# A third table for the last capped expert's rows, cleared in an earlier layer

## The reference, cut to what matters

```python
logits = jnp.einsum('bsh,eh->bse', x, router_w) + router_b        # 8 experts, 2 chosen per token
...
sorted_indices = jnp.argsort(-expert_mask, axis=0)[:cap]          # the first cap = 512 tokens of each of 7 experts
...
h = jax.nn.relu(jnp.einsum('ceh,ehi->cei', inputs, experts_inter))
out = jnp.einsum('cei,eih->ceh', h, experts_out) * in_w[..., None]
combined = jnp.zeros_like(x_flat).at[used_idx].add(out.reshape(-1, hidden))
combined = combined + x_flat * (noop_w * noop_mask)[:, None]      # expert 8 passes the token through
```

## Time and profile before

| | us |
|---|---|
| median of 3 timed runs (1227.82 to 1232.71) | 1228.27 |
| the profiled execution | 1217.18 |
| its span in the trace | 1215.4 |
| route stage, DVE's first to last instruction | 1086.63 to 1109.16 |
| capped mixture, first matmul to the end | 1110.16 to 1215.4 |
| busy in the span: PE, DVE, ACT, GpSimd | 1111.4, 997.1, 855.4, 663.5 |

### The profile page before, as it was taken

How to read it: one execution, slowest core, us unless ns; L and a number is a source line. 1 busy time by engine, 2 the same in 40 slices (tenths; PEclk the granted TensorE clock), 3 DMA queues, 4 the chain that set the end, 5 groups by cost and what they waited for, 6 DMA issues and landing times. The chain is left out here.

```text
span 1215.4 us, 33457 instructions
## 1 busy us (share of the span) xinstructions
PE 1111.4 (91%) x11747; PEld 625.7 (51%) x11747; DVE 997.1 (82%) x2703; ACT 855.4 (70%) x1830; POOL 663.5 (55%) x695
## 2 busy tenths in 40 slices
PE   4999999999999998999999998999999999937975
PEld 2344444444444444666666555655566666523752
DVE  3899999999899896689988899778999999865224
ACT  1688888888888888655556555587889999824314
POOL 3234434554333330556556567667878888735763
PEclk9999999999999999999999999998999999966998
DMA  4111111111111110000000000001122112114217
GB/s 121 32 38 40 40 39 42 41 37 40 38 42 41 43 30 14 2 2 2 1 2 1 2 2 6 24 19 47 35 53 57 53 47 55 37 64 111 53 52 205
DMA packets 83459, 48.91 MB, mean 40 GB/s; under 512 B 17431, under 2 KB 80352, under 8 KB 83296
## 3 DMA queue, kind: packets, MB, share of 16 engines
q1 hardware_dynamic: 80816, 42.62, 13.5%
q0 software_dynamic: 1792, 3.70, 1.1%
q10 hardware_dynamic: 688, 0.46, 0.1%
HBM read 16.52 MB, written 10.26 MB: 22 GB/s over the span
## 5 line engine op out<-in xcount | busy, mean ns | idle before, releaser
L627 DVE TENSOR_REDUCE mxsS<-scoreS 128x2 f32<-128x512 f32 x512 | 328.8, 685 | 38.1 <-PE scoreS L766 33.0
L515 ACT ACTIVATE PTS<-stS 128x512 f32<-128x512 f32 x512 | 283.4, 591 | 51.1 <-PE stS L770 50.5
L2014 POOL TENSOR_TENSOR ghid<-gprod,ghid 128x512 f16<-128x512 f32 x144 | 165.8, 1159 | 139.6 <-ACT ghid L2144 138.5
L766 PE MATMUL scoreS<-QK 31*128 31x256 f16 x1024 | 172.8, 279 | 23.9 <-DVE mxsS L627 11.4
L971 POOL TENSOR_TENSOR PTP<-PTP,EP 128x512 f32<-128x512 f32 x128 | 163.3, 1287 | 52.0 <-ACT PTP L1199 51.9
L770 PE MATMUL stS<-QK 32*128 32x256 f16 x1024 | 169.2, 275 | 1.3 <-ACT PTS L515 1.3
L2144 ACT ACTIVATE ghid<-gprod 128x512 f16<-128x512 f32 x144 | 90.2, 627 | 96.8 <-DVE gprod L2303 95.9
L691 PE MATMUL pvS<-PTS,Vx 128*32 128x256 f32 x2048 | 138.8, 389 | 0.5
L1372 DVE TENSOR_SCALAR AP<-score_psP 128x768 int32<-128x768 int32 x128 | 121.6, 950 | 11.6 <-PE score_psP L1528 10.7
L766 PEld LDWEIGHTS scoreS<-QK 31*128 31x128 f16 x1024 | 53.8, 93 | 145.8 <-DVE mxsS L627 94.7
L1199 ACT ACTIVATE PTP<-AP,epsP 128x768 f32<-128x768 f32 x128 | 119.2, 931 | 6.6 <-DVE AP L1372 5.9
(11 more groups left out here) (341 smaller groups left out, 2232.5 us busy)
## 6 DMA issues: line engine op xcount, KB each, us to landing
QK<-HLS SPq DMA_DIRECT2D x384, 32.0 KB, 1.9
QK<-HLP SPq DMA_DIRECT2D x192, 32.0 KB, 1.9
expert_outputs<-tzero SPq DMA_DIRECT2D x8, 512.0 KB
cgot<-expert_outputs SPq DMA_DIRECT2D x16, 256.0 KB, 5.0
tokens<-XB SPq DMA_DIRECT2D x16, 128.0 KB, 3.3
out_dram<-X SPq DMA_DIRECT2D x8, 256.0 KB, 2.3
wi<-L_ffn_experts_inter_dram SPq DMA_DIRECT2D x7, 256.0 KB, 3.1
wo<-n_L_ffn_experts_out_dram SPq DMA_DIRECT2D x7, 256.0 KB, 3.3
```

The lines of the kernel that those rows point to most:

```text
L515: act.activation(PT[:, n % NPT, :], st_ps[:, (NS * t + n) % 3, :], ACT.Exp, scale=SCALE).then_inc(s_exp, 1)
L627: dve.tensor_reduce(mxs[:, u // 4, :, at], score_ps[:, n % 2, :].rearrange("p (c s) -> p c s", c=TC), AX.X, ALU.max).then_inc(s_max, 1)
L766: scored = pe.matmul(score_ps[:, k, cols], QK[part, new, g, 0, rows], QK[part, new, g, 1, :], start=True, stop=True)
L2014: pool.tensor_tensor(hid[:, n // FC % NHID, 1, c, :], prod[:, n % NPROD, :], hid[:, n // FC % NHID, 0, c, :], ALU.subtract).then_inc(s_hid, 1)
```

## The change

The two tables become three. The scatter of the last expert (number 6 of 0 to 6) goes to the third, at row 2 x 4096 + 128 + token, whichever choice it was. All three are cleared by 24 DMAs of 256 KB from a small tile `blank`, two in each of steps 2 to 13 of the power layer, at the end of SP's step; the clears in `route` and the tile `zero` go. The first two tables are loaded when the first 24 scatters have landed, the third when the last four have. PE adds the passed tokens of blocks 0 to 5, then the first two tables of blocks 0 to 7 with the passed tokens of blocks 6 and 7 just ahead of theirs, and then the third table of blocks 0 to 7. DVE starts a block's statistics when its third table is added.

```diff
@@ power_layer, SP
+            def clear(k):
+                reach(sp, s_blank, int(k == 0))
+                at = 512 * k if k < 16 else 512 * k + P
+                sp.dma_start(od[at:at + 512, :].rearrange("(p r) d -> p (r d)", r=4), blank[:]).then_inc(s_clear, 16)
...
                 if has(t + 2):
                     spread(t + 2)
+                if 2 <= t < 14:
+                    clear(2 * t - 4)
+                    clear(2 * t - 3)
...
+            sp.wait_ge(s_clear, 16 * 24)
@@ power_layer, fixed_rows (GpSimd), called as guest (7, 9) of the layer before
+            elif k == 7:
+                pool.memset(blank[:], 0.0).then_inc(s_blank, 1)
@@ route, DVE
+               dve.tensor_scalar(third[:], who[:, 0, last], 0.5, 2.0 * NT + P, ALU.is_gt, ALU.mult),
                dve.scalar_tensor_tensor(number[:], who[:, 0, :], float(P), who[:, 1, :], ALU.mult, ALU.add))
...
-            lk(dve.tensor_copy(idx_out[:], to[:, 0, :]),
+            lk(dve.tensor_copy(idx_out[:, 0:last.start], to[:, 0, 0:last.start]),
+               dve.tensor_tensor(idx_out[:, last], to[:, 1, last], third[:], ALU.add),
                dve.tensor_scalar(idx_in[:], to[:, 1, :], float(NT - 1), None, ALU.min))
@@ route, GpSimd and SP
-            pool.memset(zero[:], 0.0).then_inc(s_zero, 1)
...
-            sp.wait_ge(s_zero, 1)
-            span = od[0:2 * NT, :].rearrange("(k p r) d -> k p (r d)", p=P, r=1024 // D)
-            for k in range(span.shape[0]):
-                sp.dma_start(span[k], zero[:]).then_inc(s_clear, 16)
             sp.wait_ge(s_weight, 1)
@@ capped_mixture, SP
-            sp.wait_ge(s_sent, 16 * TB * NX)
+            sp.wait_ge(s_sent, 16 * TB * (NX - 1))
...
+            sp.wait_ge(s_sent_last, 16 * TB)
+            rows = od[2 * NT + P:3 * NT + P, :].rearrange("(t p) d -> p t d", p=P)
+            for n in range(NBLK):
+                sp.dma_start(got[:, 2, n * TB:(n + 1) * TB, :], rows[:, n * TB:(n + 1) * TB, :]).then_inc(s_third[n], 16)
@@ capped_mixture, GpSimd, scatter
-                        .then_inc(s_sent, 16)
+                        .then_inc(s_sent if e < NX - 1 else s_sent_last, 16)
@@ capped_mixture, PE
-                    last = pe.matmul(ps[:, n, :], ident, part, start=False, stop=(c == 1))
-                last.then_inc(s_sum, 1)
+                    pe.matmul(ps[:, n, :], ident, part, start=False, stop=False)
+
+            def third(n):
+                pe.wait_ge(s_third[n], 16)
+                part = got[:, 2, TB * n:TB * n + TB, :].rearrange("p t d -> p (t d)")
+                pe.matmul(ps[:, n, :], ident, part, start=False, stop=True).then_inc(s_sum, 1)
...
-            for n in range(NBLK):
-                if n == NBLK // 2:
-                    pe.wait_ge(s_sent, 16 * TB * NX)
+            for n in range(NBLK - 2):
                 passed(n)
             for n in range(NBLK):
+                if n >= NBLK - 2:
+                    passed(n)
                 gathered(n)
+            for n in range(NBLK):
+                third(n)
```

More of the change, by code:

```diff
@@ L818, with power_layer @@
 Power = namedtuple("Power", "sync gpsimd scalar vector tensor guest_gpsimd guest_scalar guest_vector guest_tensor")
-def power_layer(nc, low, weighted_in, top, take, X, cst, cstb, QK, Vx, w, Y, chosen, router, bias, yd, wi, wo, gated, dram):
+def power_layer(nc, low, weighted_in, top, take, X, cst, cstb, QK, Vx, w, Y, chosen, router, bias, yd, od, wi, wo, gated, dram):
     NU, NE, NA, NW, WD, WU = H // 2, 4, 4, 12, 4 * P, 6 * P
@@ L880, in power_layer @@
         rnm = sb("rnm", [P, TC], F32)
+        blank = sb("blank", [P, 512], F32)
         YT = sb("YT", [P, S], F32)
@@ L918, in power_layer @@
         s_w = sem("s_w")
+        s_blank = sem("s_blank")
+        s_clear = sem("s_clear")
         s_choose = sem("s_choose")
@@ L1712, in load_weights, with route @@
         return Load(sync, gpsimd, scalar, vector, tensor, bias_tensor, s_bias, s_zero, s_one, s_set)
-def route(nc, region, cst, chosen, idx_in, idx_out, pick, noop, yd, od):
+def route(nc, region, cst, chosen, idx_in, idx_out, pick, noop, yd):
     T, LATE, BY_ACT, QUAD = NTILE, slice(NTILE - 2 * TC, NTILE), 17, NTILE // 4
@@ L1734, in route @@
         s_made = sem("s_made")
-        s_zero = sem("s_zero")
+        s_q16 = sem("s_q16")
         s_weight = sem("s_weight")
         s_found = sem("s_found")
-        s_clear = sem("s_clear")
-        zero = sb("zero", [P, 1024])
+        s_stored = sem("s_stored")
         weight = sb("weight", [P, T, 2])
@@ L1761, in route @@
         to = sb("to", [P, 2, NSLOT])
+        third = sb("third", [P, CAP // P])
         ps = ctx.enter_context(nc.psum_tensor("tps", [P, 2, 512], F32))
         block = ctx.enter_context(nc.Block())
-        HALF, FOURTH = T, T // 2
+        HALF, FOURTH, last = T, T // 2, slice(NSLOT - CAP // P, NSLOT)
         marks = {}
@@ L1794, in _ @@
             marks["found"] = lk.k
-            dve.wait_ge(s_zero, 2)
+            dve.wait_ge(s_q16, 1)
             for t in range(BY_ACT, 2 * T):
@@ L1824, in _ @@
             pool.tensor_tensor(quad[:], pair[:, :, 0, :], pair[:, :, 1, :], ALU.add).then_inc(s_made, 1)
-            pool.memset(zero[:], 0.0).then_inc(s_zero, 1)
-            pool.tensor_copy(q16[:], cst[:, C_Q:C_Q + P]).then_inc(s_zero, 1)
+            pool.tensor_copy(q16[:], cst[:, C_Q:C_Q + P]).then_inc(s_q16, 1)
             pool.wait_ge(s_v, marks["chosen", 13])
@@ L1834, in _ @@
                                    .to_broadcast([P, FOURTH, NSLOT]), ALU.mult).then_inc(s_found, 1)
-            pool.wait_ge(s_zero, 2)
         @block.scalar
@@ L1852, in _ @@
         def _(sp):
-            sp.wait_ge(s_zero, 1)
-            span = od[0:2 * NT, :].rearrange("(k p r) d -> k p (r d)", p=P, r=1024 // D)
-            for k in range(span.shape[0]):
-                sp.dma_start(span[k], zero[:]).then_inc(s_clear, 16)
             sp.wait_ge(s_weight, 1)
-            sp.dma_start(yd.rearrange("(t p) d -> p t d", p=P)[:, :, D:D + 2], weight[:]).then_inc(s_clear, 16)
-            sp.wait_ge(s_clear, 16 * (span.shape[0] + 1))
+            sp.dma_start(yd.rearrange("(t p) d -> p t d", p=P)[:, :, D:D + 2], weight[:]).then_inc(s_stored, 16)
+            sp.wait_ge(s_stored, 16)
         @block.tensor
@@ L2353, in capped_mixture @@
         res = sb("res", [P, NX, TB, D])
-        got = sb("got", [P, 2, NTILE, D])
+        got = sb("got", [P, 3, NTILE, D])
         stats = sb("stats", [P, NTILE, 6])
@@ L2378, in capped_mixture @@
         s_sent = sem("s_sent")
+        s_sent_last = sem("s_sent_last")
+        s_third = [sem(f"s_third{k}") for k in range(NBLK)]
         s_got = [sem(f"s_got{k}") for k in range(NBLK)]
@@ L2633, in build @@
             yd = nc.dram_tensor("tokens", [NT, D + 2], F32).ap()
-            od = nc.dram_tensor("expert_outputs", [2 * NT + P, D], F32).ap()
+            od = nc.dram_tensor("expert_outputs", [3 * NT + P, D], F32).ap()
             power = power_layer(nc, Region(nc, front, back), weighted_in, Region(nc, after_soft.at, region.end), take, X,
-                                cst, cstb, QK, Vx, weights[2], XB, chosen, w["router1"], w["bias1"], yd, wi, wo, gated,
+                                cst, cstb, QK, Vx, weights[2], XB, chosen, w["router1"], w["bias1"], yd, od, wi, wo, gated,
                                 dram)
@@ L2658, in _ @@
                                     (7, 1): guest("norm1", 1), (7, 4): guest("root", 2), (7, 5): guest("norm0", 2),
-                                    (7, 6): guest("norm1", 2)})
+                                    (7, 6): guest("norm1", 2), (7, 9): guest("fixed", 7)})
                 gated.drain_gpsimd(pool, 0)
@@ L2720, in build @@
         noop = region("noop", [P, NTILE], F32)
-        route(nc, Region(nc, region.at, region.end), cst, chosen, idx_in, idx_out, pick, noop, yd, od)
+        route(nc, Region(nc, region.at, region.end), cst, chosen, idx_in, idx_out, pick, noop, yd)
         region = Region(nc, region.at, nc.sbuf_usable_end)
```

## The result

Eight timed runs of each kernel, side by side: before 1228.05 us (1225.41 to 1234.29), after 1236.84 us (1234.28 to 1240.62). The ratio is 1.0074, with a 95% interval of 1.0047 to 1.0102: slower by some 8.8 us. The forecast was 1237.1.

The account below looks back on a forecast made before the run. The prediction took the tail's length as set by ACT, 1.82 us a block, and its end by when block 0 is summed. Tail +8.6, route +0.2 and power layer 0 gave 1228.27 + 8.8 = 1237.1 us, range 1230 to 1244.

Parts of the forecast that it names:

- The order of the sums: Tail: PE adds two tables for all blocks before block 0's third, so DVE's first statistics start 10.2 us later.
- Passed tokens: Tail: passed tokens of blocks 6 and 7 between the gathered sums cost PE 1.2 us (0.73 to 1.76).
- The lower clock: Tail: PE restarting at granted clock 0.50 after its pause may cost 1.55 us; none of it was taken.
- ACT's waits: Tail: DVE's and ACT's waits for loads between the first blocks go away, a gain of 1.6 us.
- Loads and scatters together: Tail: the last four scatters share DMA engines with the loads, costing 0 to 0.96 us; 0.45 was taken.
- Route: Route stage: moving the clears off SP gains nothing, and two more DVE instructions cost 0.2 us.
- Power layer: Power layer: two clears in each of twelve steps on SP cost 0, at most 11 us.
- The 11 us between profile and median: Whole kernel: the median's 11 us above the profiled execution, unexplained by any row, was put on the forecast too.
- Faster loads: Rival, tail: loads go faster while DVE and ACT rest, so PE bounds, +5.5 + 0.2, 1234.0 us; chance 0.10.
- Route's clear on the path: Rival, route's end: clears held the timed runs, so moving them gives back 8.3 us, time 1228.8; chance 0.08.
- the power layer pays: Rival, power layer: clears delay decay rows past PE's need by about 1 us in twelve steps, 1249 us; chance 0.07.
- The first sum follows the first loads: Rival, tail: the earlier start of the loads decides alone, -5.1 us, time 1223; chance 0.03.

Follow-up runs that it names:

- after_again: The changed kernel profiled once more, with no edit: one run, 1238.32 us.
- no_third_load: The changed kernel without the third table's loads, PE multiplying the first table again in their place: 1.0068 of the kernel before.
- before_again: The kernel before the change profiled once more, with no edit: one run, 1231.66 us.
- by_block: The changed kernel, passed tokens first, two tables of blocks 0 to 2, then in turn block n's third table and block n + 3's two: 1.0059 of before.
- three_early: As by_block, but third tables of blocks 0 to 2 follow the wait at once and later blocks have their three tables together: 1.0043 of before.
- clears_only: The kernel before with its two tables cleared in steps 2 to 9 of the power layer, not in route: 0.9984 of before.
- no_third: The changed kernel without the third table's loads and matmuls, all passed tokens first, last expert's rows left out: 0.9968 of before.

## Why the prediction was right

**The start of the loads.** Predicted 5.10 us earlier; 2.26 us after the 24th scatter where it was 2.27 after the 28th.

**The order of the sums.** By the forecast's terms the last gathered sum stands 19.8 + 1.2 + 0.45 = 21.45 us after the first load's start; it was 21.42, and 21.99 and 21.64 in after_again and no_third_load. The third table's first block then took 0.90 (1211.75 to 1212.65) where 0.88 was predicted. The first statistics are 10.2 us later, as forecast; the repeated pair says 9.5. no_third_load shows that neither the third table's bytes nor its waits hold anything in that order. The loads did not set the pace to the end, though: PE waited for one last at 1204.62, for block 5, and from there went on at its own 0.43 us a matmul.

```profile
1204.62 0.30 PEld L2510 LDWEIGHTS cps<-cgot,cst 128*128 128x128 f32 x2 [0.65 <-DMA cgot<-expert_outputs]
```

One reading of the prediction is off: block 0 of before was not held by its two loads. PE came to its sum straight from the passed tokens of blocks 4 to 7, without a wait for a load, in before as in before_again.

**Passed tokens.** 1.2 predicted (0.73 to 1.76), 1.3 to 1.9 measured, by one execution without them. In that one the last gathered sum stands 20.12 us after the first load's start, so 0.3 over the 19.8, where 0.45 was taken for the scatters.

**The lower clock.** The prediction took none of the 1.55 us that a slow restart of PE would cost. The granted clock stayed at 1.00 from 1186 to beyond the last sum, so nothing of it returned, and the reason given (loads still on their way) wasn't needed.

**ACT's waits.** From the first statistics to ACT's end it was 18.24 us and is 16.46: 1.8 less, where 1.6 was predicted. This holds for the shown pair only: in before_again it was 17.15, with ACT's rows 1.82 apart from the first on, so 0.7 less. What the first sum of before loses by coming later, ACT no longer waits behind it, and the two terms together are steadier than each: +10.2 - 1.8 = +8.4 and +9.5 - 0.7 = +8.8. Sum of the tail: +8.6 forecast, +8.43 and +8.80 measured. That the medians lie 8.8 us apart, to the tenth, is luck: their interval is 5.8 to 12.5 us.

**Loads and scatters together.** This is the step that failed, though it cost nothing in the changed kernel. The forecast bounded the delay at 0.96 us, by the scatters' own bytes, and put the end of their wait at no more than that later. by_block and three_early show 5.49 and 5.68 where 2.27 was: 3.2 and 3.4 us later. It is as late in the changed kernel: the last packet of GpSimd's queue there ends 4.79 us after the last scatter's start, and 1.89 in before. SP is busy with the sixteen loads until 1203.67, which covers it. The scatters don't wait for the last bytes of the loads: their packets end 4.75 to 5.66 us after the last start in all seven executions with early loads, with six loads queued or with sixteen. Packets, MB and share of 16 engines by queue in after (q0 is GpSimd's, q1 is SP's), from 1197.5 to 1198 and from 1198 to 1206:

```profile
q0 software_dynamic: 5, 0.00, 3.0%
```
```profile
q1 hardware_dynamic: 4687, 2.33, 120.4%
q8 instruction: 1, 0.02, 0.9%
```

The delay grows from scatter to scatter: in after the packets of the last four end 0.1, 1.3, 2.0 and 2.9 us later than in before, counted from the last scatter's start. That is about one load of 0.26 MB for each of the last three (0.88 to 0.96 us at the rates of the earlier trace rows, an estimate), but what sets it was not isolated. By the Trainium skill ("DMA: Bandwidth & Descriptors", Queues, rings and completion order), engines take turns between queues by packet; I had read from it that the delay is the scatters' own 0.96, and the measurement, which decides, is over three times that. Turns as such agree with the trace, as the scatters are through while loads are still queued.

**Route.** +0.2 predicted. From PE's first matmul there to its first of the capped mixture it takes 23.07 us in the shown pair both times; over all runs 22.93 to 23.07 without the third offset and 23.06 to 23.11 with it, so 0 to 0.2. DVE's last group has the two new instructions, 0.08 to 0.09 apart, as forecast:

```profile
1109.24 0.18 DVE L1826 CAST idx_out<-tto 128x24 uint32<-128x24 f32 x1
1109.33 0.15 DVE L1827 TENSOR_TENSOR idx_out<-tto,tthird 128x4 uint32<-128x4 f32 x1
1109.41 0.17 DVE L1828 TENSOR_SCALAR idx_in<-tto 128x28 uint32<-128x28 f32 x1
```

**Power layer.** 0 predicted. Two clears took SP 1.47 us in the step that was called the tightest; its decay rows went out at 987.91 and not 987.39. Counted from the start of the spread ahead of them (977.33, and 976.89 in before) that is 0.1 later, as the weights' load behind the clears took 0.43 where it had taken 1.76. clears_only shows no cost in time.

```profile
985.22 1.47 SPq L1007 DMA_DIRECT2D expert_outputs<-blankP  x2
986.73 0.43 SPq L1021 DMA_DIRECT2D wo<-n_L_ffn_experts_out_dram  x1
...
987.91 3.77 SPq L995 DMA_DIRECT2D MP<-partsP  x6
```

**The 11 us between profile and median.** They were carried over without a reason, so that the absolute 1237.1 came out is in part luck. The runs suggest a reason: PE's pauses in the capped experts, which the shown execution of before happened to lack and the nine others have. Executions without a profile don't show their stages.

**The rivals.** *Faster loads* fell: with DVE and ACT at rest 16 us of after's loads show a mean of 301 GB/s, against 288 in 16 us of before (columns as in the earlier trace rows; after, then before). That is 0.6 us for 4.19 MB, an estimate, and PE still waited for loads until 1204.62.

```profile
1192.00:1208.00 16.00, 14.39 (x32) 5.43 (x31) 0.00 (x0) 0.00 (x0) 1.82 (x2) 1.00 1.16 301
```
```profile
1185.00:1201.00 16.00, 15.57 (x35) 6.18 (x33) 8.23 (x53) 7.29 (x25) 3.57 (x3) 0.96 1.07 288
```

*Route's clear on the path* would have made clears_only up to 8.3 us faster, and *the power layer pays* would have made it slower; 0.9984 excludes each at its price, and route's unchanged length excludes that they cancel. *The first sum follows the first loads* is close to what no_third does (3.87 us after the last scatter); PE's order forbids it as long as a third table follows all the others.

## What to carry to other kernels

An earlier start is worth what the first consumer gains by it: here the loads began 5.1 us sooner, and the operand that completes block 0 was put behind all the sums of the first two tables, so the consumer began 10 us later. Before splitting a table to start early, count what the split adds per block (here a third load and two matmuls) against the slowest stage of the pipeline behind it. Compare two kernels by stages that begin and end at the same events, since one stage that varies by execution can be larger than the change.

## What was not expected of the hardware

- PE stood without any semaphore to wait for, for up to 2.53 us at a time (clears_only); in nine of ten profiled executions the capped experts took 81.1 to 86.0 us and in one 70.87. The first pause came in the same group of matmuls in all nine, the later ones at places that differ. The granted clock had a mean of 0.79 in such a stretch, so part of it passed at the lower of the two levels (1.2 of 2.4 GHz). The cause wasn't tried and stays open.
- With loads of 256 KB started 2.8 us ahead of the last scatter on the same DMA engines, the wait for the scatters ended 5.5 to 5.7 us after that scatter's start, against 2.27 alone, and the scatters' packets ended as late with sixteen loads queued as with six.
